# The second layer's quantised integers, turned by one DMA transpose a tile, with the clip on GpSimd

## The reference

```python
def act_quant(x):
    scale = 127.0 / jnp.clip(jnp.max(jnp.abs(x), axis=-1, keepdims=True), 1e-05, None)
    return jnp.clip(jnp.round(x * scale), -128.0, 127.0) / scale
...
h = x * (scale[:, None, :] * jax.lax.rsqrt(ms + EPS))
u = h @ up_w.T
val, gate = jnp.split(u, 2, axis=-1)
h = val * jax.nn.gelu(gate, approximate=False)
hq = h + jax.lax.stop_gradient(act_quant(h) - h)
wq = down_w + jax.lax.stop_gradient(weight_quant(down_w) - down_w)
y = hq @ wq.T
return y + x
```

## Time and profile before

| | us |
|---|---|
| median of three runs | 1233.23 |
| lowest and highest | 1226.01, 1234.82 |
| the profiled execution's own time | 1228.62 |
| its span in the trace | 1226.8 |
| TensorE busy | 1077.7 |
| VectorE busy | 812.8 |
| ScalarE busy | 557.8 |
| GpSimd busy | 300.3 |

### The profile page before, as it was taken

How to read it: one execution, slowest core, us unless ns; L and a number is a source line. 1 busy time by engine, 2 the same in 40 slices (tenths; PEclk the granted TensorE clock), 3 DMA queues, 4 the chain that set the end, 5 groups by cost and what they waited for, 6 DMA issues and landing times.

```text
span 1226.8 us, 19035 instructions
## 1 busy us (share of the span) xinstructions
PE 1077.7 (88%) x6775; PEld 739.2 (60%) x6775; DVE 812.8 (66%) x1613; ACT 557.8 (45%) x1242; POOL 300.3 (24%) x372
## 2 busy tenths in 40 slices
PE   6467787998989899899989989988976989999997
PEld 4312324675577467557646746753856867777775
DVE  4165556667756866775786677676443468888886
ACT  3215445655645654574566557455532332322321
POOL 0401101321321232132123213211213233333331
PEclk8757878999999999999999999998987889999999
DMA  5362624606152360634426065250040011121111
GB/s 171 77 114 51 138 49 88 128 30 135 58 100 38 98 141 17 135 75 83 64 98 131 5 132 100 58 118 2 2 150 1 28 38 53 53 63 54 53 59 36
DMA packets 87758, 92.69 MB, mean 76 GB/s; under 512 B 10241, under 2 KB 85001, under 8 KB 86641
## 3 DMA queue, kind: packets, MB, share of 16 engines
q1 hardware_dynamic: 87664, 91.49, 33.3%
HBM read 61.68 MB, written 29.78 MB: 75 GB/s over the span
## 4 chain that ended last, share of the span: by engine, by line
PE 71%; DVE 10%; DMA 6%; issue 4%; SPq 3%; POOL 3%; ACT 3%; POOLq 0%; DVEq 0%; ACTq 0%
PE gen L895 27%; PE core L895 13%; PE pvb L974 9%; PE core L948 7%; PE core L962 7%; DVE negmax L693 4%; DMA xa<-in_x_dram 3%; SPq L310 2%; PE gen L1152 2%; ACT xn L522 1%; DVE xn L669 1%; PE gen L935 1%; POOL stat L430 1%; PE pvb L1145 1%; DMA v_d<-v 1%
## 5 line engine op out<-in xcount | busy, mean ns | idle before, releaser
L693 DVE TENSOR_REDUCE negmax<-core 128x1 f32<-128x512 f32 x512 | 338.6, 685 | 216.8 <-PE core L948 214.6
L534 ACT ACTIVATE p<-core 128x512 f32<-128x512 f32 x512 | 278.2, 597 | 189.7 <-PE core L962 187.3
L948 PE MATMUL core<-kst,qst 96*128 96x512 bf16 x512 | 202.5, 413 | 60.4 <-DVE negmax L693 26.5
L895 PE MATMUL gen<-hs,wgh 128*128 128x256 f32 x1536 | 221.2, 295 | 9.1 <-DVE a L747 5.8
L895 PEld LDWEIGHTS gen<-hs,wgh 128*128 128x128 f32 x1536 | 198.4, 192 | 28.0 <-DVE a L747 9.0
L895 PE MATMUL core<-wgh,hs 128*128 128x512 f32 x768 | 193.8, 402 | 1.8 <-POOL hs L490 1.8
L450 POOL TENSOR_TENSOR a<-a 128x256 fp32r<-128x256 f32 x128 | 93.6, 731 | 333.0 <-ACT a L552 333.0
L962 PE MATMUL core<-qst,kst 99*128 99x512 bf16 x512 | 163.8, 400 | 8.0 <-ACT p L534 4.9
L895 PEld LDWEIGHTS core<-wgh,hs 128*128 128x128 f32 x768 | 140.8, 190 | 30.5 <-POOL hs L490 2.4
L948 PEld LDWEIGHTS core<-kst,qst 96*128 96x128 bf16 x512 | 47.1, 99 | 184.6 <-DVE negmax L693 80.5
L974 PE MATMUL pvb<-p,vst 128*32 128x512 f32 x1024 | 129.0, 623 | 0.0
(11 more groups left out here) (137 smaller groups left out, 1284.2 us busy)
## 6 DMA issues: line engine op xcount, KB each, us to landing
parts_d<-qk SPq DMA_DIRECT2D x32, 384.0 KB, 2.6
qst<-parts_d SPq DMA_DIRECT2D x96, 128.0 KB, 4.7
kst<-parts_d SPq DMA_DIRECT2D x96, 128.0 KB, 7.8
v_d<-v SPq DMA_DIRECT2D x8, 1024.0 KB, 11.2
vst<-v_d SPq DMA_DIRECT2D x16, 512.0 KB, 6.0
xa<-in_x_dram SPq DMA_DIRECT2D x8, 512.0 KB, 9.4
xr<-in_x_dram SPq DMA_DIRECT2D x8, 512.0 KB, 8.8
x_d<-x SPq DMA_DIRECT2D x8, 512.0 KB, 7.3
```

The lines of the kernel that those rows point to most:

```text
L534: act.activation(p32[:, ring(b, m), k * S:(k + 1) * S], stb[k], ACT.Exp, scale=SCALE).then_inc(s["exp_"], 1)
L693: dve.tensor_reduce(negmax[:, n // TT, n % TT:n % TT + 1], smb[n % 2], AX_X, ALU.max, negate=True).then_inc(s["smax"], 1)
L895: last = pe.matmul(out_, l, r, start=start and i == 0, stop=stop and i == len(passes) - 1, **kw)
L948: pe.matmul(smb[n % 2], qst[0:KROWS, h, q * P:(q + 1) * P], kst[0:KROWS, h, :], start=True, stop=True).then_inc(s["smax_mm"], 1)
```

## The change

The integers are no longer turned by TensorE into PSUM and copied out by VectorE. SyncE issues one transposing DMA a tile, from `qi` to `qT`, at the head of its step; two semaphores, one for each buffer, tell its landing. The clip, which was part of VectorE's copy, is now a pass of GpSimd over the scaled values in place, ahead of its subtraction. `down` waits for the landing; `integers` waits for the landing of the tile two before, where it waited for TensorE's turn.

```diff
@@ names of the semaphores
-... q32_ qi_ q_t q_tc d_mm final
+... q32_ qclip qi_ q_tc0 q_tc1 d_mm final
@@ SyncE, iteration_b
                 for z in range(TT):
+                    for b, t in at(z, L_QT):
+                        need_sp("qi_", TT, b, t + 1)
+                        need_sp("d_mm", TT, b, t - 1)
+                        sp.dma_start_transpose(qT[t % 2].rearrange("p (j t) -> p j t", t=P), qi[t % 2]).then_inc(s[f"q_tc{t % 2}"], 16)
                     for b, t in at(z, L_SQ3):
                         need_sp("xn3", TT, b, t + 1 - TT)
@@ GpSimd, integers
                 need(pool, "q32_", TT, b, t + 1)
-                need(pool, "q_t", TT, b, t - 1)
-                past(pool, b)
+                need(pool, f"q_tc{t % 2}", 16 * TT // 2, b, 16 * (t // 2))
+                pool.tensor_scalar(q32[t % 2], q32[t % 2], ROUND + 127.0, ROUND - 128.0, ALU.min, ALU.max).then_inc(s["qclip"], 1)
+                need(pool, "qclip", TT, b, t + 1)
                 pool.tensor_scalar(qi[t % 2], q32[t % 2], -ROUND, 1.0, ALU.add, ALU.mult).then_inc(s["qi_"], 1)
@@ VectorE
-            def q_copy(b, t):
-                need(dve, "q_t", TT, b, t + 1)
-                need(dve, "d_mm", TT, b, t - 1)
-                dve.tensor_scalar(qT[t % 2], qt_bank, 127.0, -128.0, ALU.min, ALU.max).then_inc(s["q_tc"], 1)
...
-                    for b, t in at(z, L_QT):
-                        q_copy(b, t)
@@ TensorE
-            def q_transpose(b, t):
-                need(pe, "qi_", TT, b, t + 1)
-                need(pe, "q_tc", TT, b, t)
-                for j in range(KF):
-                    last = pe.transpose(qt_bank[:, j * P:(j + 1) * P], qi[t % 2][:, j * P:(j + 1) * P], ident_bf[:, :])
-                last.then_inc(s["q_t"], 1)
...
             def down(b, t):
-                need(pe, "q_tc", TT, b, t + 1)
+                need(pe, f"q_tc{t % 2}", 16 * TT // 2, b, 16 * (t // 2 + 1))
...
-                    for b, t in at(z, L_QT):
-                        q_transpose(b, t)
```

More of the change, by code:

```diff
@@ L186, in build @@
         down_bank = gen[1][:, 0:D]
-        qt_bank = pvb[:, :].bitcast(BF16)
         XT_BANK, QK_BANK, V_BANK, OT_BANK, OP_BANK = (2, 0), (0, 1, 1, 2), (0, 2), (0, 1), (1, 2)
@@ L204, in build @@
         x2_ld0 x2_ld1 x2_ld2 x2_ld3 xr_ld0 xr_ld1 xr_ld2 xr_ld3 out_st0 out_st1 out_st2 out_st3
-        sq3 ms3 rs3 xn3 xt3 h32_3 hh3 hl3 g_mm v2_mm gelu hmul amax qscale q32_ qi_ q_t q_tc d_mm final
+        sq3 ms3 rs3 xn3 xt3 h32_3 hh3 hl3 g_mm v2_mm gelu hmul amax qscale q32_ qclip qi_ q_tc0 q_tc1 d_mm final
         """.split()
```

## The result

The changed kernel takes 1348.3 us (median of four runs, 1347.4 to 1350.1) against 1231.2 for the kernel before, measured beside it: a ratio of 1.096, 95% interval 1.091 to 1.100. The forecast was 1390, slower. A few executions of a kernel run slow as a whole (two of the six of e7_order_fused, none of the changed kernel): the ratios leave them out, the medians do not.

What follows compares the result with a forecast made beforehand. PE was taken to bound the kernel at 7.11 us a tile; the change was to make 28 circles of 12.7 us, +157, and +4.5 at the last tile: +161 on 1228.6 gives 1390 us, range 1310 to 1510.

Steps and rivals of the forecast that it cites:

- The place: SyncE's step in the second layer: xa load issues behind the transpose's wait, closing a one-tile circle of 7.7 us + R.
- The length without R: Circle from the square's start through gelus, products, maximum, scaling and clip to the subtraction's end: 7.50 us.
- R: Time from SyncE's wake for the integers to the landing of the xa load: taken as 5.0 us.
- the rival of a plain landing: xa load lands as if the transpose were a plain copy or absent: 1322 to 1340 us, slower clock 1368; chance 20%.
- The rule on transposing DMAs: Skill page's claim that transposing DMAs are as fast as plain ones; for the transpose's landing it gives 1340 us.
- PE's clock: PE, pausing each tile, may fall to its lower clock, work times 1.8; no cost at a 12.7 us period.
- the floor of 12.0 us: Least period per tile that PE at its lower clock would set if R were shorter: about 12.0 us.
- Two signs: Expected in the changed profile: PE idle about 6 us a tile; ACT's squares waiting some 7 us or more for xa.
- Down products: After the last load they wait for the transpose's landing, 7.2 us a tile; the last tile adds 4.5 us.
- 2T = 9.44 + L: Two-tile circle through the down products: T is the period per tile, L the transpose's landing time, taken as 5.0 us.
- not slower: Rival: xa loads are not held, only the transpose's landing limits; 1218 to about 1234 us, chance 6%.
- Clip on POOL: Extra GpSimd pass between scaling and subtraction, inside the circle: 1.04 us and 0.08 for its wait.

Runs made afterwards that it cites:

- e7_order_fused: Changed kernel with SyncE's xa load ahead of the transpose and GpSimd's minimum and subtraction in one pass, lower clip limit left out: 1259.3 us, ratio 1.020.
- e3_plain_copy: Changed kernel with a plain DMA of the same 256 KB in place of the transposing one, the integers left unturned: 1326.5 us, ratio 1.074.
- the ScalarE order: Changed kernel with ScalarE taking the square of tile t+3 behind the gelus of tile t, not ahead: 1319.2 us, ratio 1.066, expected about 1280.
- e1_order: Changed kernel with only SyncE's order changed, the xa load issued ahead of the transpose in each step: 1228.7 us, ratio 0.997.
- e10_order_pool: Changed kernel, full clip, with SyncE's xa load ahead of the transpose and GpSimd's low part of h ahead of 1/rms: 1219.1 us, ratio 0.993.

## Why the prediction was right, and where its size was off

- *The place.* Right: the transpose's wait for the integers of t-1, ahead of the xa load in SyncE's program, closes a circle through square and gelus. Shown by the turn of 11.22 us, by 28 waits of ACT for that DMA, and by the order alone taking the loss away.
- *The length without R.* Forecast 7.50 us from the square to the end of the subtraction; measured 1154.54 to 1162.05, 7.51. The clip was taken at 1.04 + 0.08 and measured at 1.12 from start to start.
- *R, the term that was mis-sized.* Forecast 5.0, the middle between a plain load and a price by packets; measured 1162.07 to 1165.74, 3.67: 1.24 + 0.04 of SyncE's issuing and 2.38 for the load's own landing. The transpose was priced to land at 5.0 and lands at 3.1. The 1024 small pieces are real (the queue carries 121456 packets against 87664, 1056 more a tile), but the price of each was not: the queue is busy for 34.0% of 1348.3 us against 33.3% of 1226.8, which is 1.56 us more a tile on each of the 16 DMA engines, or 0.024 us a piece, where the forecast's upper bound took 0.075. And the xa load was taken to land with the transpose because it is issued behind it; it lands some 0.6 us after it, in its usual 2.3 us from its own issue. What the transpose adds to R is the time of SyncE. 28 x (5.0 - 3.67) = 37 us of the 42 by which 1390 was too high; 28 x 0.16 = 4 are the two wakes (0.2 forecast, 0.04 measured). R = 3.67 lies barely in the forecast's band (from 3.6) and nearer to the 3.3 of the rival of a plain landing than to 5.0. The circle was read right; that its R, too, fell inside the range is owed to the width of the range.
- *The rule on transposing DMAs* (the Trainium skill, Advanced Engine Details and Errata, section X-Bar Transpose (TRN2)), by which they are as fast as plain ones: a plain copy of the same tile landed 2.3 us after its issue began, the transposing one 3.1, and the issue itself accounts for the 0.8 (1.24 against 0.47). So for the time from the end of the issue to the landing the trace agrees, 1.9 us in both. It does not agree for the DMA engines' own time: the transposing transfer takes 1.56 us of each a tile, the plain copy 0.84 (33.1% of 1315.3 us in e3_plain_copy); that cost nothing in this circle. The rule does not speak of the issuing, which is what stood in it. By the rule 1340 came out, 8 us off.
- *PE's clock.* Right that it falls and that it costs nothing here: units of 4.61 us next to ones of 3.02, clock 0.83 to 0.89, and no PE in the circle. Wrong was the floor of 12.0 us that it was to set for a shorter R, and with it the rival's 1368: the average turn is 11.16, since the 64 units take 230.5 us together, 3.6 each, and not 1.8 times their 3.02. Two signs came out smaller than announced: PE is idle for 2.6 to 3.5 us a tile (7.1 to 9.5 of 30), not 6, and a square waits 5.0 us (139.1 in 28), not 7. What releases PE was named wrongly: it is GpSimd's low part of h behind 1/rms (88.5 us), not the gelu. That cost nothing in the forecast, and 39 us in the expectation of the ScalarE order.
- *Down products.* Once the loads are out of the way, the transpose's landing is nearly hidden: by 2T = 9.44 + L and L = 3.1 it allows 6.3 us a tile, under PE's floor, and with SyncE's order mended and no clip the kernel runs at 6.62. That is what the rival *not slower* described; its condition, loads that are not held, was not met by the change and is by e1_order. The last tile pays: its down products start 3.13 us after its integers end (1340.50 to 1343.63) against 1.59; with the clip that is 2.7 us more, forecast 4.5.
- *Clip on POOL.* Forecast inside the circle at full price: right, 31 us. Not seen: with the order mended it still costs about 11 us (ratios 0.997 and 0.988), partly by way of the low part of h; only 1 us of that is the last tile's. GpSimd's order takes back about half (0.993); the rest stays, in part as waits for the turned tile.

## What to carry to other kernels

An instruction that waits, put at the head of an in-order queue, delays all that is issued behind it: before moving work to a DMA, write down what else that queue issues in the step, when each is needed, and whether the awaited thing depends on it. Here a change that frees 14 us of TensorE cost 117, and putting the xa load ahead of the transpose in the queue gave the 117 back; with GpSimd's order changed too, the kernel is 0.7% faster than before. Where a DMA stands in a circle only through what is issued behind it, as here, price it by its issuing time and by the landing of what is behind it, not by its bytes.

## What the runs showed of the hardware that was not expected

- GpSimd's two-operation pass over 128x1024 float32 takes 1.04 us for minimum with maximum and 1.05 for add with multiply, but 3.63 for minimum with add or add with minimum. (The first writes float32, the others bf16; a mixed pair that writes float32 was not run.) Fusing two passes of 1.05 into one was a loss.
- SyncE spends 1.24 us on one transposing DMA of 128x1024 bf16 and 2.50 on two of half the size, against 0.47 on a plain copy of the whole. Between these sizes the cost is by the instruction. It is not quite fixed: in e1_order the longest was 2.37 us, in e10_order_pool 2.70.
- A 128 KB load issued 1.28 us after a 256 KB transpose on the same queue lands in 2.3 us, against 2.2 in the kernel before, without a transpose.
- A transposing transfer of 256 KB takes 1.56 us of each DMA engine, a plain copy of the same bytes 0.84, although both land 1.9 us after their issue ends.
